# One maximum over two chunks, ScalarE clips behind the last square, small loads turned into columns and a split first store of the convolution kernels

## What is computed

```python
y = irfft(rfft(u_m, 2 * L) * rfft(K, 2 * L))[..., :L] + u_m * D[:, None]    # u_m: x up to each row's length
y = y * mask
xq    = clip(round(y * sqrt(7) / (mean(|y|) + eps)), -8, 7) * mean(|y|)     # per row
w_q   = clip(round(w / (mean(|w|) + eps)), -1, 1) * mean(|w|) * s           # w_gate, w_up, w_down
gate  = relu(xq @ w_q(w_gate).T) ** 2                                       # 512 -> 1376
inter = up * gate                                                           # up = xq @ w_q(w_up).T
iq    = clip(round(inter * 127 / (max(|inter|) + eps)), -128, 127) * max(|inter|) / 127
out   = x + iq @ w_q(w_down).T                                              # 1376 -> 512
```

## Time and profile before

| | us |
|---|---|
| median of 3 runs | 204.77 |
| lowest and highest | 203.62, 205.62 |
| the profiled execution | 205.15 |
| its span, from the first to the last instruction | 203.3 |

### The profile page before, as it was taken

One profiled execution on the slowest core, in us unless ns is written; L12 is line 12 of the kernel. 1 busy time (PEld: TensorE's weight loads), 2 busy tenths in 40 slices (PEclk: granted clock), 3 DMA queues, 4 the chain that ended last, 5 costly groups with the idle time before them and its releaser, 6 DMA issues.

```text
span 203.3 us, 3352 instructions
## 1 busy us (share of the span) xinstructions
PE 172.4 (85%) x1073; PEld 90.5 (45%) x1073; DVE 158.5 (78%) x426; ACT 116.2 (57%) x193; POOL 28.1 (14%) x71
## 2 busy tenths in 40 slices
PE   0001957999999869889999999999999999999992
PEld 0001935554654424344445454545454544444461
DVE  6899895457699888697779888787869698998841
ACT  2365785276999594945456381919191917244520
POOL 5014998970000000000000000000000000000000
PEclk9999999999999999999999999999999999999998
DMA  4999189879979999789557564646461526445344
GB/s 118 389 365 322 31 222 316 178 233 402 204 162 244 204 211 204 147 223 184 152 137 142 178 125 129 126 129 123 129 126 37 117 44 126 77 100 106 69 106 103
DMA packets 49487, 34.25 MB, mean 168 GB/s; under 512 B 37598, under 2 KB 37886, under 8 KB 49470
## 3 DMA queue, kind: packets, MB, share of 16 engines
q1 hardware_dynamic: 45582, 25.91, 57.1%
q10 hardware_dynamic: 3888, 8.13, 12.7%
HBM read 21.07 MB, written 4.28 MB: 125 GB/s over the span
## 4 chain that ended last, share of the span: by engine, by line
PE 56%; DVE 15%; DMA 12%; ACT 8%; issue 5%; SPq 2%; DVEq 0%; ACTq 0%
PE down_ps L646 13%; PE up_ps L613 12%; PE gate_ps L608 11%; PE conv_ps L536 6%; PE conv_ps L646 5%; PE tr_dve_ps L536 5%; DMA it_int<-inter_q 4%; DMA raw<-in_L_ffn_w_down_dram 4%; ACT g L774 2%; DVE inter L1125 2%; DVE y L1049 2%; DMA toep<-k_back 2%; ACT down_t L730 1%; PE tr_act_ps L522 1%; DMA c_in<-in_L_cond_C_dram 1%
## 5 line engine op out<-in xcount | busy, mean ns | idle before, releaser
L774 ACT ACTIVATE g<-gate_ps,gu_scale 128x416 f32<-128x416 f32 (+2 forms) x48 | 30.5, 635 | 44.4 <-PE gate_ps L608 44.4
L1125 DVE SCALAR_TENSOR_TENSOR inter<-up_ps,gu_scale,g 128x416 f32<-128x416 f32 (+2 forms) x48 | 33.3, 694 | 21.4 <-ACT g L777 21.0
L613 PE MATMUL up_ps<-up_t,q_t 128*128 128x416 bf16 (+2 forms) x192 | 45.1, 357 | 3.2 <-DVE inter L1125 3.2
L608 PE MATMUL gate_ps<-gate_t,q_t 128*128 128x416 bf16 (+2 forms) x192 | 45.2, 358 | 0.0
L1129 DVE TENSOR_REDUCE imax<-inter 128x1 f32<-128x416 f32 (+2 forms) x48 | 30.3, 631 | 1.7
L777 ACT ACTIVATE g<-g 128x416 f32<-128x416 f32 (+2 forms) x48 | 28.1, 585 | 1.5
L613 PEld LDWEIGHTS up_ps<-up_t,q_t 128*128 128x128 bf16 x192 | 18.5, 98 | 22.6 <-DVE inter L1125 4.9
L646 PE MATMUL down_ps<-down_t,i_t 128*128 128x512 bf16 (+1 forms) x121 | 27.9, 379 | 0.0
L608 PEld LDWEIGHTS gate_ps<-gate_t,q_t 128*128 128x128 bf16 x192 | 17.5, 98 | 15.7 <-issue 2.2
L536 PE MATMUL conv_ps<-toep,x_t 128*64 128x512 f32 (+3 forms) x128 | 19.0, 439 | 2.9 <-DMA toep<-k_back 2.0
L708 ACT ACTIVATE int<-raw 128x2048 bf16<-128x2048 f32 (+3 forms) x8 | 15.6, 1944 | 8.6 <-DMA raw<-in_L_ffn_w_gate_dram 5.1
(11 more groups left out here) (180 smaller groups left out, 203.3 us busy)
## 6 DMA issues: line engine op xcount, KB each, us to landing
toep<-k_back SPq DMA_DIRECT2D x16, 512.0 KB, 4.3
out_dram<-o_sb SPq DMA_DIRECT2D x30, 128.0 KB, 2.4
raw<-in_x_dram ACTq DMA_DIRECT2D x3, 512.0 KB, 9.1
raw<-in_x_dram SPq DMA_DIRECT2D x3, 512.0 KB, 8.9
raw<-in_L_ffn_w_down_dram ACTq DMA_DIRECT2D x1, 1472.0 KB, 11.9
raw<-in_L_ffn_w_down_dram ACTq DMA_DIRECT2D x1, 1280.0 KB, 8.2
raw<-in_L_ffn_w_gate_dram ACTq DMA_DIRECT2D x1, 1024.0 KB, 5.6
raw<-in_L_ffn_w_gate_dram SPq DMA_DIRECT2D x1, 1024.0 KB, 10.5
```

What stands on the lines that cost most here:

```text
L608: mm = pe.matmul(gate_ps[bank][:, 0:cn], q_t[m % 3][:, i, :], gate_t[:, i, c0:c0 + cn], start=(i == 0), stop=(i == KB - 1))
L613: mm = pe.matmul(up_ps[bank][:, 0:cn], q_t[m % 3][:, i, :], up_t[:, i, c0:c0 + cn], start=(i == 0), stop=(i == KB - 1))
L774: nc.scalar.activation(g2[bank][:, 0:cn], gate_ps[bank][:, 0:cn], ACT.Relu, scale=gu_scale[m % 4][:, 0:1]).then_inc(relu_done, 1)
L1125: v.scalar_tensor_tensor(out=inter[:, c0:c0 + cn], in0=up_ps[bank][:, 0:cn], scalar=gu_scale[m % 4][:, 1:2], in1=g2[bank][:, 0:cn], op0=AL ...
```

## The change

- `K_PARTS` has four parts in place of three: heads 0 and 1 of each half, heads 2 and 3, and the two later parts as before. `k_sums(1)` writes into the bank of `conv_ps`, the others into `tr_dve_ps`. `k_copy(0)` and the store of part 0 come ahead of the first rounding. `load_toep(0)` and `load_toep(1)` wait for the store of part 0 alone.
- The lengths and scales are loaded as single rows behind the first load of x, spread by two copies on ScalarE into four rows of 128 values, turned into four columns by four transposes on TensorE (`rest_columns`), and copied to SBUF by VectorE in one instruction.
- `turn(5)` goes behind `conv(0)` and the last two turns behind `first_q(0)`; `k_sums` of the former part 1 goes behind the first chunk's products. On VectorE `weight_copy(5)` moves behind `y_mask(0)`, `q_copy(0)` ahead of `weight_copy(7)`, and the copy of that k part behind `weight_copy(10)`.
- On ScalarE `y_sum(0)` and `y_round(0)` come ahead of `weight_copy(9)`, and ScalarE's half of the load of x tiles 4 to 7 goes behind the last `weight_copy`.
- In every tile the maximum of chunk 0 is left out, and that of chunk 1 goes over the 928 columns of both. `gamma` goes over two columns.
- In tiles 3 and 4 ScalarE's `down_copy` goes behind `relu_square(2)`.

```diff
...
         winv = sb("winv", [P, 3])
-        scl = sb("scl", [P, 3])
         wscale = sb("wscale", [P, 3])
...
-        len_i = sb("len_i", [P, 1], I32)
-        lens = sb("lens", [P, 1])
+        len_row = sb("len_row", [1, B], I32)
+        scl_row = sb("scl_row", [1, 3])
+        rest_row = sb("rest_row", [1, 4, P])
+        row_vals = sb("row_vals", [P, 4])
+        lens = row_vals[:, 0:1]
+        scl = row_vals[:, 1:4]
         x_first = sb("x_first", [P, 4 * L])
...
         rest_loaded = sem("rest_loaded")
+        rest_spread = sem("rest_spread")
+        rest_turned = sem("rest_turned")
         w_loaded = [[sem(f"w_loaded{m}{i}") for i in range(3)] for m in range(3)]
...
         stored = [sem(f"stored{p}") for p in range(2)]
-        k_stored = [sem(f"k_stored{i}") for i in range(3)]
+        k_stored = [sem(f"k_stored{i}") for i in range(4)]
         pool_step = sem("pool_step")
...
-        PAR_LOADS, REST_LOADS = 5, 5
-        K_PARTS = [(0, KH), (KH, 2 * KH), (2 * KH, HG)]
+        PAR_LOADS, REST_LOADS = 5, 4
+        K_PARTS = [(0, KH // 2), (KH // 2, KH), (KH, 2 * KH), (2 * KH, HG)]
+        def k_part(n):
+            return next(i for i, (a, b) in enumerate(K_PARTS) if a <= n < b)
+        def k_bank(i):
+            return conv_ps if i == 1 else tr_dve_ps
...
             load_half(sp, 0, 0)
+            sp.dma_start(len_row[0:1, :], length.rearrange("(a b) -> a b", a=1)).then_inc(rest_loaded, 16)
+            for i, s in enumerate((s_gate, s_up, s_down)):
+                sp.dma_start(scl_row[0:1, i:i + 1], bass.AP(s.tensor, 0, [[1, 1], [1, 1]])).then_inc(rest_loaded, 16)
...
             def load_toep(n):
-                sp.wait_ge(k_stored[min(n // KH, 2)], 16)
+                sp.wait_ge(k_stored[k_part(n)], 16)
                 wait(sp, conv_done, n - 3)
...
             store_k(0)
-            for dst, src in (
-                (len_i[0:B], length.rearrange("(b a) -> b a", a=1)),
-                (len_i[B:P], length.rearrange("(b a) -> b a", a=1)),
-                (scl[:, 0:1], bass.AP(s_gate.tensor, 0, [[0, P], [1, 1]])),
-                (scl[:, 1:2], bass.AP(s_up.tensor, 0, [[0, P], [1, 1]])),
-                (scl[:, 2:3], bass.AP(s_down.tensor, 0, [[0, P], [1, 1]])),
-            ):
-                sp.dma_start(dst, src).then_inc(rest_loaded, 16)
+            store_k(1)
             load_toep(0)
...
                 sp.wait_ge(w_rounded[1][i], rounds(1, i))
-            store_k(1)
+            store_k(2)
             load_half(sp, 2, 0)
...
                 if m == 1:
-                    store_k(2)
+                    store_k(3)
                 if m + 5 < T:
...
             u, v = o_sb[0], o_sb[1]
-            for i, (h0, h1) in enumerate(K_PARTS[1:]):
+            for i, (h0, h1) in enumerate(K_PARTS[2:]):
                 wait(pool, rest_tables, i)
...
+            def rest_columns():
+                pe.wait_ge(rest_spread, 2)
+                pe.wait_ge(winv_ready, 2)
+                for i in range(4):
+                    mm = pe.transpose(down_ps[:, 16 + i:17 + i], rest_row[0:1, i, :], ident[0:1, 0:1])
+                mm.then_inc(rest_turned, 1)
             def xt(n):
...
                 if n == AHEAD + 2:
-                    pe.wait_ge(k_ready, 3)
+                    pe.wait_ge(k_ready, 4)
                 bank = conv_bank(n)
...
                 h0, h1 = K_PARTS[i]
-                if i > 0:
-                    pe.wait_ge(rest_tables, i)
-                if i == 1:
+                if i > 1:
+                    pe.wait_ge(rest_tables, i - 1)
+                if i == 2:
                     pe.wait_ge(*copied(8))
                 for h in range(h0, h1):
-                    dst = tr_dve_ps[0:2 * JR, h * JB:(h + 1) * JB]
+                    dst = k_bank(i)[0:2 * JR, h * JB:(h + 1) * JB]
                     for c in range(2):
...
             k_sums(0)
+            k_sums(1)
             turn(0)
...
             xt(1)
-            pe.wait_ge(k_ready, 1)
+            rest_columns()
+            pe.wait_ge(k_ready, 2)
             turn(4)
-            turn(5)
             conv(0)
-            for i in range(FIRST_TURNS, len(TURNS) - 1):
+            for i in range(FIRST_TURNS - 1, len(TURNS) - 2):
                 turn(i)
             first_q(0)
-            turn(len(TURNS) - 1)
-            k_sums(1)
+            for i in range(len(TURNS) - 2, len(TURNS)):
+                turn(i)
...
                 if m == 0:
+                    k_sums(2)
                     conv(1)
...
                 if m == 1:
-                    k_sums(2)
+                    k_sums(3)
                 if m == 2:
...
                 weight_sum(m, i)
+            act.wait_ge(rest_loaded, 16 * REST_LOADS)
+            nc.scalar.copy(rest_row[0:1, 0, :].rearrange("a (g b) -> a g b", g=2),
+                           len_row[:].rearrange("a (g b) -> a g b", g=1).broadcast_to([1, 2, B])
+                           ).then_inc(rest_spread, 1)
+            nc.scalar.copy(rest_row[0:1, 1:4, :],
+                           scl_row[:].rearrange("a (i b) -> a i b", b=1).broadcast_to([1, 3, P])
+                           ).then_inc(rest_spread, 1)
             xt_copy(0)
...
             weight_copy(4)
+            y_sum(0)
+            y_round(0)
+            weight_copy(9)
+            weight_copy(8)
+            weight_copy(11)
             for i in range(3):
...
             load_half(act, 2, 1)
-            y_sum(0)
-            weight_copy(9)
-            y_round(0)
-            weight_copy(8)
-            weight_copy(11)
...
-                    act.wait_ge(k_stored[1], 16)
+                    act.wait_ge(k_stored[2], 16)
                     for i in range(3):
...
                     y_round(m + 2)
+                relu_square(2)
                 if m in (3, 4):
                     down_copy(2 * m - 5)
-                relu_square(2)
                 if m == 0:
...
                 dve.wait_ge(k_summed, i + 1)
-                bank = tr_dve_ps[0:2 * JR, :].rearrange("a (h b) -> a h b", b=JB)
+                bank = k_bank(i)[0:2 * JR, :].rearrange("a (h b) -> a h b", b=JB)
                 v.tensor_tensor(k_sb[:, h0:h1, :], bank[:, h0:h1, ::-1], d_tail[:, h0:h1, :],
...
                 wait(dve, y_rounded, n - 2)
-                v.scalar_tensor_tensor(out=y[n % 3][:], in0=steps[:], scalar=lens[:], in1=conv_bank(n)[:, ::-1],
+                v.scalar_tensor_tensor(out=y[n % 3][:], in0=steps[:], scalar=lens, in1=conv_bank(n)[:, ::-1],
                                        op0=ALU.is_lt, op1=ALU.mult).then_inc(y_masked, 1)
...
             dve.wait_ge(winv_ready, 1)
-            round_two(0, 0)
             dve.wait_ge(d_loaded, 32)
             k_copy(0)
+            round_two(0, 0)
+            k_copy(1)
             round_two(0, 2)
...
             round_two(1, 6)
-            weight_copy(5)
-            weight_round(1, 2)
-            dve.wait_ge(rest_loaded, 16 * REST_LOADS)
-            v.tensor_copy(lens[:], len_i[:])
+            dve.wait_ge(rest_turned, 1)
+            step(v.tensor_copy(row_vals[:], down_ps[:, 16:20]))
             step(v.scalar_tensor_tensor(out=wscale[:, 0:2], in0=wscale[:, 0:2], scalar=1.0 / L, in1=scl[:, 0:2],
                                         op0=ALU.mult, op1=ALU.mult))
+            weight_round(1, 2)
             y_mask(0)
+            weight_copy(5)
+            y_scale(0)
             weight_copy(6)
-            y_scale(0)
+            q_copy(0)
             weight_copy(7)
-            q_copy(0)
-            k_copy(1)
             weight_copy(10)
+            k_copy(2)
...
                                            op0=ALU.mult, op1=ALU.mult).then_inc(inter_ready, 1)
+                    if c == 0:
+                        return None
+                    first = 0 if c == 1 else c0
                     dve.wait_ge(inter_ready, NC * m + c + 1)
-                    return v.tensor_reduce(imax[:, c:c + 1], inter[:, c0:c0 + cn], AX.X, ALU.max,
+                    return v.tensor_reduce(imax[:, c - 1:c], inter[:, first:c0 + cn], AX.X, ALU.max,
                                            apply_absolute_value=True)
...
                 if m == 1:
-                    k_copy(2)
+                    k_copy(3)
                     dve.wait_ge(w_turned, len(TURNS))
...
                 step(gated(2))
-                step(v.tensor_reduce(gamma[:], imax[:], AX.X, ALU.max))
+                step(v.tensor_reduce(gamma[:], imax[:, 0:NC - 1], AX.X, ALU.max))
                 if m < 2:
...
                 else:
```

## The result

| | us |
|---|---|
| kernel before, median of 20 | 203.61 (203.07 to 205.67) |
| changed kernel, median of 20 | 202.81 (201.15 to 205.31) |
| ratio, interval | 0.9927 (0.9899 to 0.9955) |
| the changed kernel's profiled execution, its span | 201.68, 199.9 |

The change makes the kernel 0.7% faster, 1.5 us, where 2.5 us were forecast. By the medians it is 0.8 us: they hold all executions, the ratio leaves out those over 1.5% above the fastest of their kernel, six of the changed kernel's 20 and none of the other's, so it is the kinder of the two (four of the six have a mean granted clock of 0.982 or less, of which the experiments tell). The two profiled executions differ by 3.47 us, more than both. The pair overstates: later the kernel before was profiled once more, and that execution took 203.61 us.

What follows compares the result with a forecast made beforehand. Only what happens before 101 us was taken to move the end, since TensorE's matmuls fill the rest. 1.2 + 1.7 - 0.4 = 2.5 us less gave 202.3 us from the 204.77 median; range 201.0 to 204.3.

Steps and rivals of the forecast that it cites:

- second rival: DMA keeps the start's gain: x's deferred half runs before w_down, only the clips' 1.3 to 1.7 us remain; 203.4, chance 0.22.
- The split store and the small loads: At the start: Toeplitz load goes out 2.2 us after the store's issue, near 23.3, 1.6 us sooner; 0.6 with 3.16.
- VectorE behind it: Ahead of y_mask(0): VectorE's 2.0 us of room, less added copies, leaves 1.5 us; y_mask(0) near 30.15.
- The row copies and transposes: ScalarE's two copies, 1.2 us at most, fit its 1.42 us wait; nothing if the loads land by 23 us.
- From y_mask(0) to conv(1): y_round(0) moves with y_mask(0); k_sums now stands behind the products, so the gain counted at conv(1) is 1.5 us.
- What w_down keeps back: w_down's load goes out 0.8 to 1.5 us sooner; 1.2 of the start's 1.5 us carried through (bounds 0 and 1.5).
- The maxima and the clips: Tiles 3 and 4: product of chunk 2 comes 0.85 us sooner in each, 1.7 us; 928-column maximum takes 1.12 us.
- Later tiles: Longer maximum costs nothing, or 0.3 us in tile 15; 0.4 us (0 to 0.8) given back at tile 4's transpose.

Runs made afterwards that it cites:

- after_again: The changed kernel run and profiled once more, with no edit: 202.39 us, ratio 0.9940 (0.9908 to 0.9971).
- after_max_apart: The changed kernel with a separate maximum for each chunk, as before the change: 201.39 us, ratio 0.9886 (0.9839 to 0.9932).

## Why the prediction was right or wrong

Direction and range held (202.81 in 201.0 to 204.3); the size was forecast as 2.5 us and measured as 1.5, or 1.2% and 0.7%. That the time itself came within 0.5 us of the 202.3 forecast is luck in part: the forecast was taken from a median of three, 204.77, and that of 20 is 203.61, 1.2 us lower. The gain of 1.5 us lies outside the forecast's own 1.9 to 3.1 us and where the second rival (chance 0.22) had it, 1.3 to 1.7 us less what a later wait takes. By its own steps:

- **The split store and the small loads.** The Toeplitz load should go out 2.2 us after the store. It went out after 1.5 to 3.1 us. I had bounded this from one trace in which the small loads hid it. It depends on when the first loads end: 1.88 us where w_up's second part was there by 19.4 us, 3.12 where it came at 20.8, 1.64 with 256 KB fewer, 1.53 where the store itself went out later. The upper bound of 3.16 us was a real case.
- **VectorE behind it, 1.5 us.** True in the first profile pair once the tables' 0.65 us are taken off (29.45 against 31.67), and 0.7 us on the mean of five. What is late there in most profiles is the path by x, w_up's sum, mean and rounding, which the change leaves as it was; the old order had 1.35 us of idle time that covered its scatter. In the two latest, `after_again` and `after_max_apart`, it is conv(0), and not for the Toeplitz load: it starts at 28.94 and 28.04 straight behind TensorE's slow transposes. In five of the eight profiles conv(0) doesn't wait for that load at all. The working had no term for TensorE there.
- **The row copies and transposes.** 0.28 and 0.50 us, in the wait, as told. In `after_again` they put xt_copy(0) off by some 0.3 us, but ScalarE waits for 1.27 us before its next copy of x.
- **From y_mask(0) to conv(1).** Held: 5.9 us in the changed kernel (29.45 to 35.37) and 6.2 before.
- **What w_down keeps back.** This step failed. I carried 1.2 us of the start through it, and the start alone shows 0.4 (ratio 0.9981, interval 0.9952 to 1.0010), with nothing left at tile 2 on the mean of five profiles. The load was issued sooner and landed no sooner, as the second rival has it; but not by that rival's mechanism, as x's half put back changes nothing. The store near 36 us holds x's half and a Toeplitz load back, the DMA idles ahead of it and has the same bytes to move behind it. With those bytes ahead of the store w_down came 1.2 us sooner in one profile, where the wait for the transpose of tile 1 took it, and 2.1 us sooner against the tables in the other, where most of it reached tile 2; and the DMA then idles behind the store in place of ahead of it. No run shows it in the time, so that this is the whole of what holds the start's gain back stays open.
- **The maxima and the clips.** 1.7 less 0.4 us forecast; 1.6 us measured alone (0.9920). (The working has 1.27 us for the wait in tile 3 where the row has 1.23, so 0.80 us a tile and not 0.85.) The maximum of 928 columns takes 1.120 us, as the line through the two others gave. The product of tile 3 came 0.88 us sooner, against inter_q of tile 2 (7.11 us behind it before, 6.23 now). I had the price of the joint maximum in the sum (0.43 us a tile) without saying what follows from it: that the change would do better without it: 201.39 us, and 0.75 us less from tile 2 to tile 4 in the trace.
- **Later tiles.** 0.4 us given back at the transpose of tile 4: 0.27 us in the first pair of profiles (1.52 less 1.25), but the wait is 1.40 us in the second profile of before and 0.79 to 2.08 us in the six others with the new start and the moved clips, so this term isn't told from nothing. Tile 15 cost nothing: from its last product to the end of the span it takes 13.0 us, and 13.3 before.
- **What I had not seen** is the granted clock. No term of the sum stands for it, but 18 of 32 executions of the changed kernel lose some clock, and its median of 20 stands 1 us above the 201.82 of its nine executions at 0.997 or more. Why it falls more often there than in the kernel before, whose wait in tile 3 is as long (1.60 and 1.64 us in the first profiles), stays open.

## What to carry to other kernels

A gain at the start has to be followed to the first place where a transfer of fixed volume must have landed; asking for it sooner may be worth nothing if the DMA then idles ahead of something else that hasn't moved. An engine's operation with much to cover it belongs behind the short one that another engine waits for; here that exchange of lines alone brought 2.4 us, more than the whole change. Two traces of one kernel differ by as much as such edits bring (1.5 us in both kernels here), so a saving must be shown to hold over several of them, or measured by stages against a mark of the same trace.

## What the runs showed of the hardware

A store of 10 KB to device memory had landed 1.5 to 3.1 us after its issue in eight profiles, the later the more of the first loads was still under way. TensorE's granted clock fell from 1.0 to 0.5 (2.4 to 1.2 GHz) behind a stretch in which it was busy for 1.63 of 4 us, and stayed there for 3 to 7 us in three profiles although TensorE was then busy nearly all the time. Such a stretch alone doesn't decide it: in the first profile of the changed kernel TensorE was busy for 1.39 us of the 4 us from 68 to 72, in that of the kernel before for 1.43 of the 4 us from 70 to 74, and the clock stayed at 1.00. The changed kernel's executions with a mean clock of 0.98 (0.02 of 200 us, at half the clock some 8 us) took 2.4 us more than those at full clock, those with 0.99 (some 4 us) 0.6 us more, and 1.5 us in the kernel before; the microseconds at half clock are estimates from the mean clock. And at the very start eight transposes took 1.03 us or 0.61 us while the granted clock in the rows was 1.00 in both cases, so the granted clock of the rows doesn't tell all of TensorE's rate.
